# Fourth batch unit's values matmul moved behind the next tile's cross-attention query product, on another PSUM bank

## What is computed

```
scores = einsum('bshd,bthd->bhst', qh, kh) / sqrt(d)      # h = 16 heads, d = 16, t = 257 rows of context
attn = softmax(scores)
ctx = einsum('bhst,bthd->bshd', attn, vh)
x = x + ctx.reshape(b, sq, e) @ wo.T + bo                 # _layernorm of x is the query
```

## Time and profile before

| | before |
|---|---|
| time, median of 3 runs | 1462.64 us (1462.29 to 1463.04) |
| the profiled execution's own time | 1460.61 us |
| its span, first to last instruction | 1458.8 us |
| TensorE matmuls busy | 1364.2 us, 94% |
| VectorE busy | 872.8 us, 60% |
| ScalarE busy | 817.4 us, 56% |
| GpSimd busy | 651.4 us, 45% |
| mean granted TensorE clock | 0.987 of full speed |

### The profile page before, as it was taken

The page is one execution under the profiler, slowest core; times in us unless marked ns, Lnnn a source line. Parts: engine busy times, 40 slices in busy tenths (PEclk is TensorE's granted clock), DMA queues, the critical chain, the costliest instruction groups (busy, mean ns, idle before and its releaser), DMA issues. The chain is left out here.

```text
span 1458.8 us, 51913 instructions
## 1 busy us (share of the span) xinstructions
PE 1364.2 (94%) x19870; PEld 1132.7 (78%) x19903; DVE 872.8 (60%) x3111; ACT 817.4 (56%) x2335; POOL 651.4 (45%) x1195
## 2 busy tenths in 40 slices
PE   8789999999998999999999987899999999999996
PEld 6467777777776777777777755799999999999996
DVE  5668888888887888998889876333111111111111
ACT  1478888888887888888888876321111111111110
POOL 2234444444455455455455444356544444444442
PEclk9799999999999999999999999999999999999999
DMA  9323433434333233333333224566666666665662
GB/s 330 139 71 90 120 100 113 119 94 118 100 114 112 86 111 114 93 108 111 100 103 101 72 70 169 186 181 181 176 181 182 189 180 181 182 181 178 184 183 66
DMA packets 91183, 199.44 MB, mean 137 GB/s; under 512 B 13568, under 2 KB 48128, under 8 KB 79840
## 3 DMA queue, kind: packets, MB, share of 16 engines
q1 hardware_dynamic: 72304, 174.61, 37.3%
q0 software_dynamic: 15680, 18.69, 7.2%
q10 hardware_dynamic: 2992, 3.28, 0.7%
HBM read 178.52 MB, written 18.29 MB: 135 GB/s over the span
## 5 line engine op out<-in xcount | busy, mean ns | idle before, releaser
L2156 ACT ACTIVATE heT<-ps 128x512 f32<-128x512 f32 x142 | 84.7, 597 | 412.0 <-PE ps L2082 393.2
L1414 ACT ACTIVATE x_prob<-ps,x_nmax 128x257 f32<-128x257 f32 x512 | 238.0, 473 | 66.2 <-DVE x_nmax L1775 61.1
L2082 PEld LDWEIGHTS ps<-xeT,w_block 128*128 128x128 f32 x2272 | 264.6, 192 | 3.7 <-issue 0.2
L2082 PE MATMUL ps<-xeT,w_block 128*128 128x128 f32 x2272 | 266.1, 275 | 0.0
L2069 PE MATMUL ps<-contexts,heT 128*128 x1136 | 257.5, 379 | 1.6 <-DVE ye L1965 1.6
L2069 PEld LDWEIGHTS ps<-contexts,heT 128*128 128x128 f32 x1136 | 210.1, 190 | 27.5 <-issue 2.0
L1775 DVE TENSOR_REDUCE x_nmax<-ps 128x2 f32<-128x514 f32 x256 | 169.1, 681 | 25.1 <-PE ps L1242 23.7
L1250 PE MATMUL ps<-constants,x_prob 128*128 128x128 f32 x1024 | 156.2, 281 | 23.7 <-ACT x_prob L1414 22.3
L1250 PEld LDWEIGHTS ps<-constants,x_prob 128*128 128x128 f32 x1024 | 116.8, 143 | 46.8 <-ACT x_prob L1414 38.6
L1418 ACT ACTIVATE x_probT<-ps 128x512 f32<-128x512 f32 x256 | 148.1, 626 | 8.5 <-PE ps L1250 7.7
L1964 DVE COPY to_ix<-places 128x1 uint32 x71 | 10.9, 154 | 231.3 <-PE ps L2069 222.8
(11 more groups left out here) (280 smaller groups left out, 2740.9 us busy)
## 6 DMA issues: line engine op xcount, KB each, us to landing
w_block<-in_m_w SPq DMA_DIRECT2D x71, 1024.0 KB
contexts<-in_cT SPq DMA_DIRECT2D x112, 257.0 KB
contexts<-in_cn SPq DMA_DIRECT2D x112, 256.0 KB
contexts<-in_m_w SPq DMA_DIRECT2D x8, 1024.0 KB
contexts<-in_cT SPq DMA_DIRECT2D x4, 1028.0 KB
xin<-in_x SPq DMA_DIRECT2D x32, 128.0 KB, 2.1
lastq<-in_lastq SPq DMA_DIRECT2D x32, 128.0 KB, 2.2
contexts<-in_cn SPq DMA_DIRECT2D x4, 1024.0 KB
```

What stands on the lines that cost most here:

```text
L1414: A(p1[u % 2][:, r, :], ps[:, r, 0:KEYS], ACT.Exp, bias=nmax1[u % 2][:, r:r + 1], accum_out=rsum1[u % 2][:, r:r + 1]).then_inc(e1_ok.handl ...
L2082: t = mm(ps[:, half, at:at + P], w1[b][:, k, f * P:(f + 1) * P], xeT[b][:, k, :], start=k == 0, stop=k == H - 1)
L2156: A(heT[b][:, half * FK // 2:(half + 1) * FK // 2, :].rearrange("p k t -> p (k t)"), ps[:, half, :], ACT.Gelu).then_inc(heT_ok.handle, 1)
```

## The change

`unit_values(s, 3)` leaves its place directly behind `unit_values(s, 2)` on TensorE and goes behind `c0_q(s + 4)`, and it writes bank 4 in the place of bank 5. The steps that depend on it move too: `unit_own(s, 3)`, `unit_turned(s, 3)` on VectorE, `unit_scaled(s + 1, 3)` on GpSimd. With them `s1_turned` goes ahead of `unit_max(s + 1, 1, 0)`, `s1_values` ahead of `s1_out`, the indirect DMAs wait for unit 2 instead of unit 3, and `s1_qT` of the last tile but one is done in the stack phase.

The banks, and what the closing tiles leave over:

```diff
-         "s1_q": 4, "ff_up0": 6, "ff_up1": 7, "V2": 6, "V3": 5, "s1_v_scores": 7, "c0_norm_T": 6, "s0_norm_T": 5, "c0_q": 6,
+         "s1_q": 4, "ff_up0": 6, "ff_up1": 7, "V2": 6, "V3": 4, "s1_v_scores": 7, "c0_norm_T": 6, "s0_norm_T": 5, "c0_q": 6,
...
-    CLOSING = {"s1_v_scores": 2, "s1_values": 2, "s1_out": 1, "s1_norm_T": 1, "ro_norm_T": 3, "s1_q": 1, "s1_qT": 2, "s1_masked": 2, "s1_turned": 2, "s1_inv": 2, "ro_norm": 3, "s1_x5": 2,
+    CLOSING = {"s1_v_scores": 2, "s1_values": 2, "s1_out": 1, "s1_norm_T": 1, "ro_norm_T": 3, "s1_q": 1, "s1_qT": 1, "s1_masked": 2, "s1_turned": 2, "s1_inv": 2, "ro_norm": 3, "s1_x5": 2,
```

What TensorE waits for, and its order:

```diff
             def s0_norm_T(t):
                 W(pe, norm_s["self0"], t, "norm")
-                W_bank(pe, (t - 3, (o1_ok, 4)))
...
             def unit_values(t, u):
                 if u == 0:
-                    W_bank(pe, (t + 2, (dve_s["self0"], "masked")), (t - 1, (o1_ok, 4)))
+                    W_bank(pe, (t + 2, (dve_s["self0"], "masked")), (t - 1, (o1_ok, 1)))
...
                 if u == 3:
-                    W_bank(pe, (t + 3, (dve_s["cross0"], "x")), (t, (o1_ok, 1)))
+                    W_bank(pe, (t - 1, (dve_s["self1"], "q")), (t + 2, (dve_s["self0"], "x")))
...
                 at(s, unit_values, 2)
-                at(s, unit_values, 3)
                 at(s - 1, s1_v_scores)
                 at(s + 4, c0_norm_T)
                 at(s + 1, unit_probs_T, 0, 0)
                 at(s + 3, s0_norm_T)
                 at(s + 1, unit_probs_T, 0, 1)
                 at(s + 4, c0_q)
+                at(s, unit_values, 3)
                 at(s + 1, unit_scores, 1)
                 at(s + 3, s0_qkv)
+                at(s - 1, s1_values)
                 at(s, s1_out)
-                at(s - 1, s1_values)
                 at(s + 1, unit_probs_T, 1, 0)
```

GpSimd:

```diff
                 at(s + 1, unit_scaled, 2)
-                at(s + 1, unit_scaled, 3)
-                scatter_behind(s, s + 1, 3)
+                scatter_behind(s, s + 1, 2)
                 at(s + 2, unit_last, 0)
                 at(s + 2, q1_bias)
                 at(s, s1_bias)
...
                 at(s + 5, c0_bias)
+                at(s + 1, unit_scaled, 3)
                 at(s + 2, unit_last, 1)
```

VectorE, in the loop and, last, in the expert phase:

```diff
                 at(s, unit_own, 2)
-                at(s, unit_own, 3)
                 at(s + 2, ff_hidden_scale)
                 at(s, unit_turned, 2)
                 at(s - 1, s1_masked)
...
                 at(s + 2, ff_quantise_hidden)
+                at(s - 1, s1_turned)
+                at(s, unit_own, 3)
                 at(s + 1, unit_max, 1, 0)
-                at(s, unit_turned, 3)
-                at(s - 1, s1_turned)
                 routing(s - 1, 5)
                 at(s + 1, unit_max, 1, 1)
+                at(s, unit_turned, 3)
                 at(s - 1, s1_inv)
...
-            s1_qT(tiles - 2)
             rows_copy(0, 0)
```

## The result

The changed kernel takes 1470.44 us, median of 7 runs (1468.62 to 1475.47), beside 1462.36 for the kernel before in the same comparison (1459.22 to 1463.21). The ratio is 1.005, 95% interval 1.003 to 1.0069; measured once more it was 1.0043 (1.0029 to 1.0058). So it is slower by 0.4 to 0.5%. That lies inside the predicted range of 1457 to 1471, but only 0.6 us from its end and above the forecast's own range, which ended at 1467; the sum said +0.9 us, and the two comparisons gave +8.1 and +6.5. The range held because rival 1 (1472) had stretched it, not because the sum was right. The profiled execution took 1468.8 us, its span is 1466.9, 8.1 more than before.

The account below looks back on a forecast made before the run. It took a loop of waits between TensorE, VectorE and ScalarE to bound the kernel. Early +2.9, long -4.3, later +2.5 and ends -0.2 gave +0.9 us on 1462.64, about 1463.6 us; range 1457 to 1471 for 8 in 10.

Parts of the forecast that it names:

- the forecast's own range: Whole kernel: the main case without the rivals was to land between 1460.5 and 1467 us, chance 0.47.
- the sum: Whole kernel: early, long and later rounds and the ends together were to add +0.9 us.
- rival 1: VectorE's chain doesn't shorten and the later rounds see no relief: +9.7 us, about 1472; chance 0.20.
- The early rounds: Twelve rounds without indirect DMAs: turning 3 delays s1_out and the hidden transposes by 0.24 us each, +2.9 us.
- The late load: Last quarter's load, some 6 us later, stays hidden; as a rival, landing after 268 costs +28 us, 1491; chance 0.03.
- The long rounds: Five long rounds: parting two adjacent units ends TensorE's pauses, read as instruction fetch; -4.3 us.
- The later rounds: Sixteen rounds with indirect DMAs: relief of VectorE's scaling in twelve, -1.2, and losses in four, +3.7; together +2.5 us.
- the fourth ones: Four later rounds, every fourth: x_bias now falls together with VectorE's scaling, +0.9 us each with the later s1_out.
- The bound for this case: Later rounds: relief in none, and two additions to wait for in the four, +7 us.
- The other bound: Later rounds: relief of VectorE's scaling in all sixteen, -3 us.
- Rival 3: Relief in all sixteen later rounds, early cost only 0.1 us each from TensorE's spare time: -6.1 us, 1456.5; chance 0.18.
- rival 2: TensorE's pauses are not instruction fetch, or come back at the new place: +5.2 us, 1467.8; chance 0.12.

Follow-up runs that it names:

- e6: Changed kernel with unit_turned 3 ahead of the second half of unit_max on VectorE and unit_scaled 3 ahead of c0_bias on GpSimd; ratio to the kernel before 1.0034.
- e4: Changed kernel with the load of a context's last quarter cut to 16 of 128 partitions; ratio to the kernel before 1.0056.
- e1: Changed kernel with GpSimd's two small router steps ahead of its three wide bias additions; 1461.22 us, ratio to the kernel before 1.0006.
- e5: Changed kernel with GpSimd's two small router steps between the wide additions x_bias and self_x_bias; 1462.23 us, ratio to the kernel before 0.9991.
- e8: Changed kernel with one more GpSimd instruction of 0.27 us, a copy of unit 2's scaling, ahead of the indirect DMAs; ratio to the kernel before 1.0063.
- c1: Kernel before with GpSimd's small router steps ahead of its wide additions and unit 3's values behind s1_v_scores; ratio to the kernel before 0.9952.
- e3: Kernel before with unit 3's values behind s1_v_scores instead of directly behind unit 2's values; 1447.93 us, ratio 0.9913.
- e7: Kernel before with unit 3's values behind s1_v_scores, indirect DMAs waiting for unit 2, and unit 3's scaling behind two wide GpSimd additions; 1480.16 us, ratio 1.0125.
- e2: Kernel before with GpSimd's two small router steps ahead of its wide bias additions; 1450.16 us, ratio 0.9931.
- c3: Kernel before with unit 3's values behind s1_v_scores and VectorE's unit_own 3 behind s1_masked; 1505.68 us, ratio 1.0292.

## Why the prediction was right and wrong

**The early rounds** (+0.24 each): the steps came to within 0.05 us: L844 at 0.30, the first half of `unit_max` at 8.39 us (forecast 8.35), turning 3 at 9.59 (9.56), `s1_out` at 9.87 (9.85). The hidden transposes are 0.16 us later than before, not 0.24, for two reasons. `s1_out` has no wait: TensorE is dense, and what decides is TensorE alone, not turning 3, which is ready 0.05 us earlier. e6 bears it out: with `x_outT` early, these rounds stay at 26.13. And `s1_out` with both transposes takes 1.87 us (265.23 to 267.10), where the sum had 0.98 + 0.50 + 0.49.

**The late load** (hidden, about 1 us left; lands by 266): wrong. It was a rival with 0.03 at 1 us in every round, and came as 0.1 to 0.8 us in four early rounds, 1.4 us in all, by e4. The forecast had the quarter issued 10.0 us into the round (263.5 in the round from 253.46) and landed at 12.5 (266). In the changed kernel the three pieces are out at 10.2 (265.56 in the round from 255.36); but DMA is busy longer, in the round from 281.55 it goes quiet at about 294.6, 13.0 us in, and `c0_scores` starts at 296.03. So the landing was put too early and the margin of 1 us wasn't there. With 1.4 of this, ten rounds at 0.15 and 0.7 for the round from 123.90, the early part is 3.6 us instead of 2.9.

**The long rounds** (-4.3): right in size. No row of unit values behind 100 us in the changed kernel's trace has a pause ahead; the five rounds took 27.24 each, no longer than their neighbours, so what set them apart, 137.62 - 5 x 26.67 = 4.3, is gone. They gained only 1.4 us because the step below put 0.57 back on each. That the pauses end when the runs stand as far apart as in the change is shown: e1, e4, e5, e6 and e8, which keep its order on TensorE, have none either in these rounds. That the distance sets their length is borne out only in part: in the same round it was 1.54, 0.46 and 0.23 with growing distance, but c1, with e3's order, has up to 1.44. That it is instruction fetch is still argued. The Trainium skill (Runtime: NRT & Kernel Launch, instruction fetch mechanics) says that crossings of a block are mostly hidden; if these pauses are such crossings, here they were not.

**The later rounds** (+2.5): this is the step that failed. "In twelve rounds `x_bias` then starts 0.2 us ahead of VectorE's step, which I expect to wait for one addition instead of two: done 0.9 us sooner." It started 0.09 ahead (the change moved it by 0.13 us, not 0.27), and VectorE waited for both additions, 1.89 us. e5 shows that it is the second addition, directly behind the first, that takes the expected relief away: with a small step between them the scaling waits for one, 1.20. It isn't shown why VectorE doesn't get in between the two here and does in the early rounds (261.33). So the ordinary rounds got the later `s1_out` (+0.39, forecast +0.4) and no relief (0, forecast -0.5), and the fourth ones +1.3 instead of +0.9. Against a kernel without pauses the sixteen rounds cost 1.2 + 2.9 + 5.3, about 9.3 us, instead of 2.5. The bound for this case stood at +7, and that was an error of adding up: without relief the prediction's own terms give 12 x 0.4 + 3.7 = 8.5, before anything for a second addition. The other bound, -3, doesn't follow from them either.

I had also read the earlier trace rows too quickly. The Trainium skill (SBUF — State Buffer, who interferes with whom) says that the shared port goes to whoever issues first, for the whole instruction, and I held 686.72 against it. But another GpSimd step, `x_lastv` (128x64), runs directly ahead of `x_bias`: in that round from 686.51 to 686.82, so GpSimd was first. The same holds for 637.98 above. A row in which VectorE is first is in the changed kernel's last round but one, timeline of VectorE and GpSimd:

```profile
855.62 2.28 DVE L1736 TENSOR_SCALAR ffn_hidden<-ffn_hidden,ffn_qscale 128x1024 f32<-128x1024 f32 x1
855.68 0.31 POOL L1536 TENSOR_TENSOR x_lastv<-contexts,x_prob 128x64 f32<-128x64 f32 x1
855.93 0.73 POOL L903 TENSOR_TENSOR x_bias<-x,r_x_bo 128x256 f32<-128x256 f32 x1
```

The third step is `self_x_bias`, from 856.61 to 857.34. VectorE starts 0.06 us ahead of the first of the three and still waits until all are over. By the starts of the rows the trace doesn't agree with the rule; whether they show who issued first, no run here settles.

**Sum:** +3.6 - 4.3 + 9.3 - 0.5 = +8.1, the difference of the spans. That the measured time still lies in the range for 8 in 10 is luck as far as the later rounds go: their term was off by 6.8 us, and the right -4.3 beside it kept the total just inside. Rival 1 was nearest, and half right: the later rounds saw no relief; but L844 did shorten, to 0.30. Rival 3's thought for the early rounds, that TensorE's spare time is all that counts, was right as well, with 0.15 us a round and not its 0.1. Of rival 2, that the pauses come back at the new place is out; whether they are fetch isn't decided.

What stays open: why VectorE and ScalarE see TensorE late in e7, what the pauses are, and when GpSimd lets VectorE in between two steps. e3's gain away from the pauses is not open: the nine rounds from 595.56 us, which have none, give 5.3 us, all of it in the seven in which the kernel before has the bad phase; GpSimd's reorder alone gave 4.3 in the same nine (e2).

## What to carry to other kernels

Ask of a moved step what phase it gives to an engine that only waits for it: here the wait of an indirect DMA set when three wide GpSimd additions met VectorE, and that was worth more than the move itself. Price a chain of such meetings as a whole, since a collision that is avoided in one place came back at the next in e1, e5 and e8. And a wait that an instruction carries for a bank's reader is part of its price, as c3 shows.

## What the hardware did that I had not expected

- A 128x1024 scaling on VectorE takes 0.74 us beside a small GpSimd step, 1.20 when it starts inside one wide GpSimd addition (128x256, 0.73), and 1.89 to 2.28 when it loses to two such additions. Where it lost, it was through 0.56 to 0.57 us after the last addition ended (612.22 above, 609.65 in e5, 857.34 in the changed kernel). I had expected it to be let in after each addition.
- Which engine wins doesn't follow from the distance of the two starts. VectorE won with 0.17 us (261.33) and with 0.24 (637.17 in e8) ahead of a wide addition, and lost with 0.04 (637.98) and with 0.31 (855.62). In the rows in which it won the addition took about 1.2 us.
- A small step can pay as much as a large one: a cast of 8 columns took 0.75 us beside such an addition (612.04 in e5), and 0.31 when the addition was nearly over. The `unit_max` reductions, which read PSUM, took 0.65 to 0.69 us in every trace, beside GpSimd or not.
- VectorE can see TensorE's result 2.8 us after the matmul's row ends, and ScalarE another one 2.4 us after, without a pause in TensorE's rows (e7). The end of such a row is modelled, and in e7 it isn't the time at which others could go on.
